# Last chunk of a two-layer mixture kernel: the last expert's part is added in a different form

## The reference

```python
combined = concat([nx, evidence, anchor], axis=-1)
router_probs = softmax(combined @ router_W + router_b)            # 3 experts
h = silu(einsum('btc,ecr->bter', combined, e_w1) + e_b1)          # 3 x 512 hidden features
expert_out = einsum('bter,erh->bteh', h, e_w2) + e_b2
routed = sum(expert_out * router_probs[..., None], axis=-2)
g = sigmoid(silu(combined @ gate_w1 + gate_b1) @ gate_w2 + gate_b2)
return x + g * (routed @ out_w + out_b)
```

## Time and profile before

| | us |
|---|---|
| median of the three runs shown | 491.77 |
| lowest and highest | 491.24, 493.49 |
| the profiled execution, its own time | 490.68 |
| span in its trace | 488.90 |
| PE busy | 455.2 (93% of the span) |
| DVE busy | 319.1 (65%) |
| ACT busy | 192.7 (39%) |
| POOL busy | 138.3 (28%) |

### The profile page before, as it was taken

One profiled execution on the slowest core, in us unless ns is written; L12 is line 12 of the kernel. 1 busy time (PEld: TensorE's weight loads), 2 busy tenths in 40 slices (PEclk: granted clock), 3 DMA queues, 4 the chain that ended last, 5 costly groups with the idle time before them and its releaser, 6 DMA issues.

```text
span 488.9 us, 6881 instructions
## 1 busy us (share of the span) xinstructions
PE 455.2 (93%) x2418; PEld 358.0 (73%) x2418; DVE 319.1 (65%) x797; ACT 192.7 (39%) x331; POOL 138.3 (28%) x208
## 2 busy tenths in 40 slices
PE   3966999999999999999978999999999999999994
PEld 3654676776766757766456888888888888888883
DVE  4779785478457646657878468765786757843345
ACT  4931343335333533444532344523454344432210
POOL 2074084007002200200006223263333533325333
PEclk9978999999999999999989999999999999999999
DMA  8801004400010101000020000001000010001001
GB/s 290 324 0 44 1 21 144 160 0 23 23 43 2 39 5 44 1 0 2 0 62 9 1 1 1 1 1 44 1 0 2 2 43 2 0 2 43 1 1 43
DMA packets 7314, 17.45 MB, mean 36 GB/s; under 512 B 880, under 2 KB 2288, under 8 KB 7152
## 3 DMA queue, kind: packets, MB, share of 16 engines
q1 hardware_dynamic: 5040, 11.57, 6.7%
q10 hardware_dynamic: 1584, 3.15, 1.7%
q0 software_dynamic: 656, 2.29, 1.7%
HBM read 14.45 MB, written 2.10 MB: 34 GB/s over the span
## 4 chain that ended last, share of the span: by engine, by line
PE 85%; DVE 6%; ACT 3%; issue 2%; DMA 1%; POOL 1%; POOLq 0%; SPq 0%; DVEq 0%; ACTq 0%
PE bank L1125 54%; PE pair L1125 14%; PE pair L1218 4%; PE bank L1260 3%; PE bank L1257 3%; DMA wss_sb<-in_wss 1%; PE bank L1226 1%; DVE lnt L792 1%; PE bank L1270 1%; ACT keys L613 1%; DVE keys L870 1%; PE bank L1281 1%; DVE nm L909 1%; PE bank L1366 1%; DVE vtail L889 1%
## 5 line engine op out<-in xcount | busy, mean ns | idle before, releaser
L579 POOL TENSOR_TENSOR hs<-hid,hs 128x512 fp32r<-128x512 f32 x48 | 64.2, 1338 | 124.3 <-DVE hs L1078 124.3
L1125 PE MATMUL bank<-nx,w1h 128*128 128x512 f32 x224 | 74.2, 413 | 0.0
L1125 PE MATMUL pair<-w2h,hs 128*128 128x256 f32 x384 | 70.2, 281 | 0.0
L737 ACT ACTIVATE hid<-bank,ab 128x512 f32<-128x512 f32 x48 | 33.1, 689 | 88.3 <-PE bank L1125 88.2
L1125 PEld LDWEIGHTS pair<-w2h,hs 128*128 128x128 f32 x384 | 62.4, 189 | 4.3 <-POOL hs L579 0.2
L909 DVE TENSOR_REDUCE nm<-pair 128x4 fp32r<-128x616 f32 x64 | 51.2, 800 | 20.3 <-PE pair L1218 19.2
L666 ACT ACTIVATE pt<-bank 128x512 f32<-128x512 f32 x80 | 47.5, 600 | 29.0 <-PE bank L1125 26.3
L1078 DVE CAST hs<-hid 128x512 fp32r<-128x512 f32 x48 | 20.5, 428 | 57.1 <-ACT hid L737 56.3
L1125 PE MATMUL pair<-w2l,hs 128*128 128x256 f32 x192 | 54.1, 282 | 0.0
L1125 PEld LDWEIGHTS bank<-nx,w1h 128*128 128x128 f32 x224 | 39.6, 190 | 6.2
L1125 PE MATMUL bank<-nx,w1l 128*128 128x512 f32 x112 | 44.1, 394 | 0.0
(11 more groups left out here) (190 smaller groups left out, 911.5 us busy)
## 6 DMA issues: line engine op xcount, KB each, us to landing
stage<-in_w1n POOLq DMA_DIRECT2D x7, 256.0 KB, 3.3
w1e_sb<-in_w1e SPq DMA_DIRECT2D x1, 1792.0 KB, 6.8
x_sb<-in_x SPq DMA_DIRECT2D x3, 512.0 KB, 14.7
stage<-in_w1a SPq DMA_DIRECT2D x3, 512.0 KB, 5.8
stage<-in_ew2T SPq DMA_DIRECT2D x3, 512.0 KB, 3.9
out_x<-x_sb SPq DMA_DIRECT2D x3, 512.0 KB, 2.7
wss_sb<-in_wss SPq DMA_DIRECT2D x2, 512.0 KB, 8.6
x_sb<-in_x ACTq DMA_DIRECT2D x1, 512.0 KB, 4.9
```

What stands on the lines that cost most here:

```text
L579: g_.tensor_tensor(hs[:, q % 3, 1, :], hid[:, q % 2, :], hs[:, q % 3, 0, :], ALU.subtract).then_inc(hl_r, 1)
L737: A(dst, B_H[n % 2][:, :], ACT.Silu, bias=ab1[:, m, c // CPB:c // CPB + 1]).then_inc(h_r, 1)
L1125: ins = mm(dst, a, b_, start=first and i == 0, stop=last and i == len(terms) - 1, skip_group_check=free)
```

## The change

Only the last chunk (`c = NC - 1 = 3`) is treated differently, and of it only the last expert. With `q2 = p_2 * y` the product of the last expert, the kernel before forms `(th + 1) * (base + q2)` and adds it to `x`. The changed kernel splits this:

- `scale` (DVE, new, four instructions, at blocks 0 to 3 of the last chunk): `lsc[j] = (th[j] + 1) * p_2`, in a new SBUF tensor of 4 KB a partition that takes the rest of the room kept for `place`.
- The last expert's `bias` moves from block 10 to block 5.
- `gated` (at block 8 for tiles 0 and 1, at block 9 for 2 and 3): DVE forms `acc[j] = (th[j] + 1) * acc[j]`, where `acc` now holds everything but the last expert's product, and POOL adds it into `x` (`base_ready`).
- `last` (after block 11, for each tile): DVE forms `acc[j] = y_tile(j) * lsc[j]`, POOL adds it into `x`, SP stores. It waits for `last_y_mm`, which PE now counts once for each row tile of the last `part`; DVE waits until both tiles of a bank are done (`j + 2 - j % 2`), and for `scale` and `gated` of that tile.
- The `sum` and `final` of the last expert in the last chunk are gone.

```diff
@@ -143,6 +143,7 @@
         acc = sb("acc", (P, TJ, D), F32, late)
         gz = sb("gz", (P, 2, D), F32, late)
         th = sb("th", (P, TJ, D), F32, late)
+        lsc = sb("lsc", (P, TJ, D), F32, late)
         late.close()
         sb("place", (P, KC, W1N))
 
@@ -257,6 +258,7 @@
         h_mm, h_r, g_mm, gz_r, th_r = sem("h_mm"), sem("h_ready"), sem("g_mm"), sem("gz_ready"), sem("th_ready")
         w2_r, hh_r, hl_r = sem("w2_split"), sem("hidden_hi"), sem("hidden_lo")
         y_mm, y_r, f_r, o_r = sem("y_mm"), sem("y_used"), sem("delta_ready"), sem("out_ready")
+        y_l, base_r, scale_r, last_r = sem("last_y_mm"), sem("base_ready"), sem("last_scale_ready"), sem("last_ready")
         rg_r, rs_r = sem("rsqrt_guess"), sem("rsqrt_ready")
         dch, pch = sem("vector_chain"), sem("pool_chain")
 
@@ -390,13 +392,21 @@
             def products(c, m):
 
                 yield ("part", c, m)
-                if m % 4 == 2:
+                if m % 4 == 2 and (c, m) != (NC - 1, HB - 2):
                     yield ("bias", c, m // 4)
-                if m % 4 == 3:
+                if (c, m) == (NC - 1, 5):
+                    yield ("bias", c, E - 1)
+                if c == NC - 1 and m in (8, 9):
+                    for j in (0, 1) if m == 8 else (2, 3):
+                        yield ("gated", j)
+                if c == NC - 1 and m < TJ:
+                    yield ("scale", m)
+                if (c, m) == (NC - 1, HB - 1):
+                    for j in range(TJ):
+                        yield ("last", j)
+                elif m % 4 == 3:
                     for j in range(TJ):
                         yield ("sum", c, m // 4, j)
-                        if (c, m) == (NC - 1, HB - 1):
-                            yield ("final", TJ * c + j)
 
             for c in range(NC):
                 take = front1(c + 1) if c + 1 < NC else iter(())
@@ -583,7 +593,19 @@
                 pool.wait_ge(f_r, n + 1)
                 g_.tensor_tensor(x[:, n, :], x[:, n, :], acc[:, n % TJ, :], ALU.add).then_inc(o_r, 1)
 
-            walk(l1_steps(), {"hsplit": hsplit, "final": final, "ln_stats": lambda c: newton(NC + c)})
+            def gated(j):
+
+                n = TJ * (NC - 1) + j
+                pool.wait_ge(f_r, n + 1)
+                g_.tensor_tensor(x[:, n, :], x[:, n, :], acc[:, j, :], ALU.add).then_inc(base_r, 1)
+
+            def last(j):
+
+                n = TJ * (NC - 1) + j
+                pool.wait_ge(last_r, j + 1)
+                g_.tensor_tensor(x[:, n, :], x[:, n, :], acc[:, j, :], ALU.add).then_inc(o_r, 1)
+
+            walk(l1_steps(), {"hsplit": hsplit, "final": final, "gated": gated, "last": last, "ln_stats": lambda c: newton(NC + c)})
 
 
         @block.scalar
@@ -1102,13 +1124,30 @@
                 dve.wait_ge(th_r, n + 1)
                 V.scalar_tensor_tensor(acc[:, j, :], th[:, j, :], 1.0, acc[:, j, :], ALU.add, ALU.mult).then_inc(f_r, 1)
 
+            def scale(j):
+
+                dve.wait_ge(th_r, TJ * (NC - 1) + j + 1)
+                V.tensor_scalar(lsc[:, j, :], th[:, j, :], 1.0, pr[:, (NC - 1) % 2, j, E - 1:E], ALU.add, ALU.mult).then_inc(scale_r, 1)
+
+            def gated(j):
+
+                dve.wait_ge(y_r, TJ * (E * NC - 2) + j + 1)
+                V.scalar_tensor_tensor(acc[:, j, :], th[:, j, :], 1.0, acc[:, j, :], ALU.add, ALU.mult).then_inc(f_r, 1)
+
+            def last(j):
+
+                dve.wait_ge(y_l, j + 2 - j % 2)
+                dve.wait_ge(scale_r, j + 1)
+                dve.wait_ge(base_r, j + 1)
+                V.tensor_tensor(acc[:, j, :], y_tile(j), lsc[:, j, :], ALU.mult).then_inc(last_r, 1)
+
             front_parts = {"ln_stats": ln_stats, "ln": ln, "nxf": nxsplit, "score": score, "weights": weights, "wsplit": wsplit,
                            "router": router}
             out_parts = {"uz": uz, "wp": wproj, "m_taken": mpiece}
             walk(l0_steps(), {"val": val, "place": place, "stats": chunk_stats, "rsqrt": chunk_rsqrt, "norm": norm, "split": xsplit, "rows": rows, "shift": shift, "prep": prep,
                               **out_parts, **front_parts})
             walk(between_steps(), {**out_parts, **front_parts})
-            walk(l1_steps(), {"gate": gate, "w2_split": w2_split, "hsplit": hsplit, "bias": bias, "sum": expert_sum, "final": final, **front_parts})
+            walk(l1_steps(), {"gate": gate, "w2_split": w2_split, "hsplit": hsplit, "bias": bias, "sum": expert_sum, "final": final, "scale": scale, "gated": gated, "last": last, **front_parts})
 
 
         @block.tensor
@@ -1427,7 +1466,10 @@
                     hi, lo = hs[:, q % 3, 0, P * j:P * j + P], hs[:, q % 3, 1, P * j:P * j + P]
                     ins = passes(y_tile(j), [(hi, w2h[:, m, :]), (lo, w2h[:, m, :]), (hi, w2l[:, m, :])],
                                  first=r == 0 and j % 2 == 0, last=r == 3, free=True)
-                ins.then_inc(y_mm, 1)
+                    if q == HB * NC - 1:
+                        ins.then_inc(y_l, 1)
+                if q < HB * NC - 1:
+                    ins.then_inc(y_mm, 1)
 
             rows_parts = {"uz": uz, "zt": ztr, "wp": wproj, "m": mpiece}
             front_parts = {"nxt": nxt, "score": score, "wtr": wtr}
```

## The result

| | kernel before | changed kernel |
|---|---|---|
| median, us (runs) | 492.78 (10) | 488.71 (10) |
| lowest and highest | 491.24, 495.47 | 487.55, 490.26 |
| profiled execution, its own time | 490.68 | 489.15 |
| span in its trace | 488.9 | 487.3 |

The ratio of the times is 0.9913, with a 95% interval of 0.9886 to 0.9941: faster, by 2.9 to 5.6 us. The forecast was 489.4 in a range of 488.0 to 491.4, a gain of 2.3 us. So the time fell into the range, and the gain came out larger than the forecast gain: 4.1 us between these medians, and still 3.1 us against the 491.77 on which the forecast stood. Whether that is more than the scatter of this kernel had to be settled.

A forecast was written before the change was run, and what follows sets the result against it. PE was taken to bound the kernel until 481.65 us, then DVE and POOL. A tail gain of 2.3, other edits at nothing, gave 488.4 from the profiled 490.68 and 489.5 from the median 491.77; predicted 489.4, range 488.0 to 491.4.

The forecast's parts named there:

- What bounds the kernel, and that only the tail counts: Whole span: PE alone sets the end until 481.65 us, then DVE and POOL; the change mainly shortens that 7.27 us tail.
- The sum of the tail: After PE's last product: one DVE product, four POOL additions at 0.70; last addition ends 484.36 against 486.73, 2.37 us gained.
- the allowance of 0.07: POOL's start in the tail: middle taken between 2.37 us gained and a tail 0.14 later, giving 2.3.
- Is POOL free in time?: Behind the split of block 11: POOL finishes its two base additions at 481.54, or the whole tail is 0.14 later.
- the first course of the two: Behind the split of block 11: waiting `gated` 3 goes before POOL's additions, ends 480.18; POOL free at 481.54, gain 2.37.
- The early row of a DVE instruction that waited through several additions: Early in the span: small DVE instruction issued at 37.4 took 1.99 us beside four POOL additions; spoke for the second course.
- `last` and POOL's additions don't hold each other up: Tail: DVE's product of PSUM and SBUF operands runs beside POOL unhindered, 0.42 for one product, 0.70 for an addition.
- rival 2: Tail: tiles don't flow; DVE starts late, 0.7 longer, 490.1; mutual shut-out, step 1.14, 490.7. Chance 0.16, same.
- The edits costed at nothing: Last chunk: moved bias (2.7 us into 3.32 idle), `scale` (0.54 each), tile counts (0 to 0.1), early `gated` (upper end 0.3).
- Rival 1: More than counted: block 11's split takes 1.30, PE's last part starts 0.16 earlier; gain 2.5 us, 489.3. Chance 0.18, faster.
- Rival 3: Slower: POOL's additions for tiles 0 and 1 outlast 478.44, delaying block 11's split and PE's last part. Chance 0.04.
- one sign of being wrong: Whole kernel: the prediction is wrong if, among other signs, the median moves by over 2.6 us.

## Why the prediction held, and where it was off

*What bounds the kernel, and that only the tail counts.* Right. The declarations alone changed nothing, and the times of the changed kernel, taken together, give the ratio that the tail gives.

*The sum of the tail.* From the last cast, forecast (kernel before at 477.93) and measured:

| | forecast | measured |
|---|---|---|
| PE's last part starts | 2.02 | 1.96 |
| first product on DVE | 3.11 | 2.97 |
| first last addition on POOL | 3.61 | 3.48 |
| end of the last addition | 6.43 to 6.57 | 6.25 |
| end of the span | 8.60 to 8.74 | 8.34 |

The mechanism was right, and the gain was forecast 0.3 too small, in four small terms of the same sign and the allowance of 0.07 that is spoken of below. The split beside the first `gated` took 1.40 and not the 1.46 that it took beside a bias update (0.06). DVE starts 0.03 behind PE's tile and not 0.11 (0.08). POOL's pace was 0.69 and not 0.70, and its additions took 2.77 together, not 2.82 (0.05). From the last addition to the end it was 2.09, not 2.17 (0.08). That 0.3 carried the gain over the bound of 0.5% (2.46 us): the forecast had put "within 0.5%" ahead of "faster", at 0.56 to 0.40, because of 0.16 us. The pooled times (0.9942 to 0.9951) lie on that bound.

*Is POOL free in time?* Right, and by the first course of the two. The second `gated` on DVE:

```profile
479.64 1.51 DVE L1135 SCALAR_TENSOR_TENSOR acc<-th,acc 128x256 f32<-128x256 f32 x1
```

It ends at 481.15, 0.28 behind the split's end (480.87), and POOL's next addition was the one held up (0.92 of the pair's 1.62). The waiting DVE instruction went first, as the page of the Trainium skill has it (SBUF — State Buffer, "Who interferes with whom": issue order decides). The early row of a DVE instruction that waited through several additions was the wrong precedent to lean on; half of the difference of 0.14 was allowed for it and was not needed. Why that one waited longer was not tried. "In time" was by nothing to spare: POOL came free within 0.02 us of the moment at which DVE's product let it begin.

*`last` and POOL's additions don't hold each other up.* Right: 0.37 for a product (1.47 for the four), 0.69 for an addition, both running. So the step of 1.14 of rival 2 did not come.

*The edits costed at nothing.* Right as far as the traces show. Two of the four `scale` instructions, and the first expert's bias between them:

```profile
442.98 0.35 DVE L1130 TENSOR_SCALAR lsc<-th,pr 128x256 f32<-128x256 f32 x1
...
452.20 2.15 DVE L1109 TENSOR_SCALAR acc<-b,pr 128x256 f32<-128x256 f32 x4
454.39 0.35 DVE L1130 TENSOR_SCALAR lsc<-th,pr 128x256 f32<-128x256 f32 x1
```

They take 0.35 each where the row gave 0.54. Two of them had a price that the prediction did not see: they push a `final` of the chunk before beside a POOL split, and it takes 1.50 instead of 0.42 (at 443.24 and at 447.85). Nobody waited for it: from the cast at 442.63 to the one at 456.47 it is 13.84 us, as in the kernel before (441.60 to 455.44). The additions for tiles 0 and 1 ended 0.78 before the split of block 11. The moved bias fits.

*The rivals.* Rival 1 (more than counted, 2.5 us) came nearest to the tail measured, though not by its mechanism: the split was 1.40, not 1.30. The short split came in every kernel in which DVE did no gated or bias instruction beside it (1.26 to 1.29 in five runs); with the bias moved alone it was worth 0.28, in the others the cast or POOL itself was late. Rival 2's first half is the run that waits for all tiles: 0.76, forecast 0.7. Rival 3 is real (0.97 us when provoked) and was absent.

*The signs, and the range.* The traces show what was named: POOL's last additions 0.69 apart, beginning 0.16 before PE's last product ends (482.60), the last of them ending 2.6 behind it (forecast 2.8, before 5.1), and the second `gated` at 1.51. But one sign of being wrong did appear: the median moved by more than 2.6 us, by 3.1 against the 491.77 of the forecast. The repeats show that as scatter (all 30 times against the 69 put the medians 2.4 us apart), so the sign was set narrower than medians of three and ten executions allow. That this first median fell into the range is owed to the width given for scatter, and in part to luck; that the tail shrank by 2.6 is not.

## What to carry to other kernels

When the last dependent step of an output is `f(base + last part)` and `f` is linear, apply it to the base and to the last part's factor while the matrix engine is still busy; then cost the tail by the slowest engine that remains, here POOL at 0.69 us a tile. Before moving base work in front of it, find which short instruction on the chain runs beside it: two base additions on POOL ended 0.78 us before they would have been in the way, four cost 1 us, and moving them a block sooner only moved the hold-up from the split to the cast. An engine that takes work off the slowest one can also bring the stores so close together that they take back part of the gain (0.44 of 0.75 us here). Read a gain of this size from a stretch between two instructions that both kernels share, not from spans or from one ratio.

## What the runs showed of the hardware

Times of one and the same program on one chip lie up to 6.5 us apart (the kernel before: 489.34 to 495.84), in groups, and the traces say where. PE is busy throughout from 124 to 144 us, in the first layer, with the same instructions to do in all kernels (at a lower clock fewer of them fall into the same 20 us, x95 instead of x116); the granted clock there (third column from the right) was 1.00 in the trace of before, 0.91 in that of after and 0.74 in the run with the signals alone:

```profile
124.00:144.00 20.00, 20.00 (x116) 15.43 (x114) 8.86 (x15) 8.72 (x15) 0.00 (x0) 1.00 0.14 40
```

```profile
124.00:144.00 20.00, 20.00 (x110) 16.03 (x109) 8.16 (x14) 7.99 (x14) 0.00 (x0) 0.91 0.14 40
```

```profile
124.00:144.00 20.00, 20.00 (x95) 15.44 (x91) 5.87 (x10) 5.57 (x9) 0.00 (x0) 0.74 0.14 40
...
132.00:140.00 8.00, 8.00 (x30) 5.57 (x28) 2.57 (x4) 1.79 (x3) 0.00 (x0) 0.50 0.22 67
```

ACT's eighth output of the first layer followed its seventh by 11.89, 13.17 and 16.33 us in these three, and in all other traces by one of these three values (to 0.02). The last row, of 132 to 140 us of that run, has 0.50: the lower level of 1.2 GHz, granted while PE was busy throughout. The stretch costs 0, 1.3 or 4.4 us: nothing, half of what the whole change brings in the tail, or more than all of it. It does not go with the change: of fourteen traces eight have it at 11.9, four at 13.2 (the changed kernel's first among them) and two at 16.3 (the signals alone, and one of the versions beyond the change), and all these kernels are alike up to the last chunk. Beyond that, the first such output comes between 54.0 and 56.8 us, a spread that arises ahead of it. Why the clock falls in some executions only was not tried.

A part of the first set's large gain comes from this. Of the 99 executions of the kernel before in the later sets, 13 have a mean granted clock of 0.967, and they take 494.7 to 495.9 us. Of the 20 later ones of the changed kernel three have 0.969 or 0.970, and they take 492.9 to 493.0. In the first set three of the ten times of the kernel before are 495.0 or more, while none of the changed kernel's ten has a clock below 0.976 or a time above 490.3: the slow group fell on one side only.
